# Linear output moved from routing to in front of the last projection, both it and the experts unrolled, first loads reordered

## The chip, the cores and the metric

The kernel runs on one core of a Trainium2 chip. The metric is the device time of one execution in microseconds. The kernel before takes 3159.98 us, the median of three runs from 3156.24 to 3162.64.

## The reference, cut to what matters

Two layers work on x, 4096 tokens (2 sequences of 2048) of 256 features.

```python
xn = layernorm(x)
# layer 0: linear attention beside a transformer block with experts
q_feat, k_feat = elu(rope(q) * hd**-0.5) + 1, elu(rope(k)) + 1
kv, k_sum = einsum('bhtd,bhtv->bhdv', k_feat, v), k_feat.sum(axis=2)
denom = maximum(einsum('bhtd,bhd->bht', q_feat, k_sum), 1e-6)
s = (einsum('bhtd,bhdv->bhtv', q_feat, kv) / denom[..., None]) @ W_out   # the "linear output"
#   the block: causal softmax attention (16 heads of 16), then 8 experts, two for a token,
#   1024 rows each: exp_out = gelu(rows @ W1 + b1) @ W2 + b2
g = silu(x1 + gate0 * exp_out[row0] + gate1 * exp_out[row1])
x = x + s * g
# layer 1: causal softmax attention with heads of 32 beside a quantised linear map
xn = layernorm(x)
s = attention(xn @ Wq, xn @ Wk, xn @ Wv) @ Wo
g = silu(xn @ int4(kernel) + bias + (xn @ a) @ b)
out = x + s * g
```

## The kernel before, in words

Tokens lie on the 128 partitions in 32 tiles, and a block is 4 tiles (512 tokens), so there are 8 blocks. A matrix product needs the features on the partitions, so rows are turned on TensorE first and evicted from PSUM by ScalarE. Stages follow one another, each its own block of the program: at its end all engines meet at a barrier, and POOL first drains its own queue (line 40).

1. `project_first` (tiles `pr_`, 0 to 269 us): layer norm, the linear attention's q, k, v, its features (`qf_all`, kept on the chip) and sums (`kv_sum`), and q, k, v of layer 0's softmax attention. Everything is unrolled and every engine follows a list of names (`pe_names`, `act_names`, `dve_names`). PSUM tiles of two banks come in turn from a ring of 3, and transposes (`Txn`, `Tz`, `soft`) from one more, `rot`. `Txn 0` can't start before ScalarE has copied the tables "soft cos", "soft sin" and "soft neg" out of `rot`. Statistics of the rows are taken in three groups of blocks: 0, then 1 to 3, then 4 to 7, the last of these in block 1.
2. `narrow_attention` (269 to 1095), `project_and_gate` (1099 to 1167).
3. `route_and_linear` (tiles `rl_`, 1167 to 1256.6): VectorE works out, in one chain, for each of 8 x 1024 expert rows which token it holds (`rows_at`). Between its links stand 16 calls of `normalise`, one for each pair of tiles of the linear output (10 ahead of `rows_at`, 6 behind it). For a pair, TensorE makes the numerators (`num`), VectorE divides by the denominators (L2125 is the first of its instructions), TensorE turns the result (`tr`, L2239), ScalarE copies it to `nT` (L2103), TensorE multiplies by W_out (`out`, L2251), ScalarE copies that, SyncE stores it in DRAM (`s_out`). Once `rows_at` is there (L2214), POOL issues 16 gathers (L2007) for experts 0 and 1.
4. `experts` (`ex_`, 1256.6 to 1738.1): loops over pairs of experts. For one: T (transposes of its rows, by halves of 4 tiles) into `xT`, h (8 x 2 products and gelu on ScalarE), y (128 products), an add on VectorE (L2401), and a store of POOL to `exp_out`, which POOL waits for.
5. `combine_and_project` (`p_`, 1738.2 to 2022): a loop over blocks. The expert rows of a block are gathered (L2545), mixed with the gates on VectorE (L2610, L2614), silu on ScalarE, times s (loaded back from `s_out`), plus x, layer norm, then TensorE's T (L2698), q and k (L2705), v (L2711) and y (L2718). q and k leave PSUM twice: the high half by ScalarE (L2577), the low half by VectorE (L2666). PSUM is a ring of 8 banks. `xT` is one buffer.
6. `wide_attention` (2022 to 3083.8) and `finish` (to 3153.7).

The names of steps carry block numbers, and an engine waits for another by the name of the step.

## Time and profile before

| what | us |
|---|---|
| median of 3 runs | 3159.98 (3156.24 to 3162.64) |
| the profiled execution's own time | 3155.44 |
| its span, first to last instruction | 3153.7 |
| TensorE busy | 2875.4 (91%) |
| VectorE / ScalarE / POOL busy | 2034.5 / 1545.4 / 953.3 |
| granted TensorE clock, mean | 0.951 of full |

A time in the rows below is read from the start of the span. `[3.63 <-ACT p_xT L2567]` behind an instruction says that its engine had been idle for 3.63 us, and what ended it. One line of a timeline can hold several instructions (x32), with the duration of all. PEclk is the granted TensorE clock: 1.00 is 2.4 GHz, 0.50 is 1.2 GHz.

### The profile page before, as it was taken

How to read it: one execution, taken by the hardware profiler on the slowest of the kernel's cores; microseconds unless marked ns; L12 is line 12 of the kernel's file. 1: busy time of each engine (PE TensorE's matmuls, PEld its weight loads, DVE VectorE, ACT ScalarE, POOL GpSimd, SP SyncE). 2: the span in 40 equal slices, each digit the busy share in tenths (PEclk: the TensorE clock that was granted, in tenths of full speed). 3: DMA queues.
4: the chain of work that ended last, by engine and by line, in shares of the span. 5: the costliest groups of instructions: out<-in, count | busy, mean ns of one | idle time of the engine just before them, and what ended most of it. 6: DMA issues, size and time to landing. Idle time of an engine off the chain costs nothing. (4 is left out here: it accounts for less than half of the span.)

```text
span 3153.7 us, 47934 instructions
## 1 busy us (share of the span) xinstructions
PE 2875.4 (91%) x18023; PEld 1334.8 (42%) x18023; DVE 2034.5 (65%) x4568; ACT 1545.4 (49%) x2562; POOL 953.3 (30%) x452
## 2 busy tenths in 40 slices
PE   7998999999999877999998588799999999999987
PEld 4664333333333256566666244323333333333326
DVE  6776899988999366000000465588877877878823
ACT  2442477776777732222221344344566565565560
POOL 0001000000000021211200221056777777777790
PEclk9997899999999978999999799889999999999998
DMA  4223121112220053222210445430220220202005
GB/s 121 84 64 88 34 45 42 23 37 45 48 42 15 23 160 98 66 61 68 85 47 20 145 148 185 125 71 5 64 61 8 65 50 22 61 21 55 8 8 173
DMA packets 149886, 204.29 MB, mean 65 GB/s; under 512 B 18224, under 2 KB 113280, under 8 KB 147744
## 3 DMA queue, kind: packets, MB, share of 16 engines
q1 hardware_dynamic: 129904, 170.76, 19.7%
q0 software_dynamic: 8704, 25.18, 3.0%
q10 hardware_dynamic: 11072, 5.60, 0.7%
q8 instruction: 130, 2.13, 0.3%
q14 instruction: 76, 0.62, 0.1%
HBM read 121.01 MB, written 79.95 MB: 64 GB/s over the span
## 5 line engine op out<-in xcount | busy, mean ns | idle before, releaser
L912 ACT ACTIVATE at_probs<-at_st 128x512 f32<-128x512 f32 (+3 forms) x1280 | 588.6, 541 | 446.0 <-PE at_st L998 283.9
L874 POOL TENSOR_TENSOR at_probs<-at_probs 128x2048 f32<-128x2048 f32 (+3 forms) x208 | 732.8, 3528 | 222.6 <-ACT at_probs L912 136.8
L383 DVE TENSOR_REDUCE at_part<-at_s 128x1 f32<-128x512 f32 (+3 forms) x1280 | 689.7, 603 | 69.9 <-PE at_s L421 31.7
L365 ACT ACTIVATE at_probs<-at_st 128x1024 f32<-128x1024 f32 (+3 forms) x640 | 541.5, 895 | 277.4 <-PE at_st L440 140.3
L938 DVE TENSOR_REDUCE at_part<-at_s 128x1 f32<-128x512 f32 x768 | 498.8, 683 | 69.0 <-PE at_s L990 65.0
L990 PE MATMUL at_s<-at_kT,at_qT 96*128 96x512 f16 (+3 forms) x1280 | 392.0, 362 | 28.4 <-DMA at_kT<-klo 10.4
L998 PE MATMUL at_st<-at_qT,at_kT 98*128 98x512 f16 (+3 forms) x1280 | 379.8, 356 | 15.4 <-ACT at_probs L912 10.7
L421 PE MATMUL at_s<-at_kT,at_qT 48*128 48x512 f16 (+3 forms) x1280 | 360.5, 367 | 26.1 <-DMA at_kT<-klo 9.8
L932 DVE CUSTOM_DVE_ANT_0 at_s<-at_s,at_later 128x384 f32<-128x384 f32 (+3 forms) x512 | 247.0, 498 | 110.1 <-PE at_s L990 109.7
L507 PE MATMUL at_acc<-at_probs,at_v 128*32 128x512 f32 (+3 forms) x2560 | 305.2, 551 | 8.9 <-ACT at_otile L352 8.8
L2401 DVE TENSOR_TENSOR ex_ot<-ex_bank,lin_b 128x512 f32<-128x512 f32 x32 | 22.1, 692 | 449.0 <-PE ex_bank L2431 449.0
L1059 PE MATMUL at_acc<-at_probs,at_v 128*32 128x512 f32 (+3 forms) x2560 | 288.4, 538 | 6.4 <-ACT at_otile L894 6.2
L440 PE MATMUL at_st<-at_qT,at_kT 50*128 50x512 f16 (+3 forms) x1280 | 283.0, 357 | 5.0 <-ACT at_probs L365 3.3
L1859 POOL TENSOR_TENSOR ag_a<-ag_a,ag_r 128x1024 f32<-128x1024 f32 x8 | 18.8, 2360 | 851.5 <-ACT ag_r L1876 851.5
L990 PEld LDWEIGHTS at_s<-at_kT,at_qT 96*128 96x128 f16 x1280 | 110.1, 98 | 355.6 <-DVE at_part L938 151.4
L421 PEld LDWEIGHTS at_s<-at_kT,at_qT 48*128 48x128 f16 x1280 | 100.1, 94 | 370.8 <-DVE at_part L383 317.7
L2431 PE MATMUL ex_bank<-lin_w,ex_hT 128*128 128x256 f32 x1024 | 224.5, 380 | 7.0 <-ACT ex_hT L2383 7.0
L2422 PE MATMUL ex_bank<-ex_xT,lin_w 128*128 128x512 f32 x512 | 223.7, 595 | 1.6 <-ACT ex_xT L2375 1.6
L2431 PEld LDWEIGHTS ex_bank<-lin_w,ex_hT 128*128 128x128 f32 x1024 | 193.9, 190 | 43.0 <-ACT ex_hT L2383 13.8
L998 PEld LDWEIGHTS at_st<-at_qT,at_kT 98*128 98x128 f16 x1280 | 123.0, 98 | 186.4 <-ACT at_probs L912 106.8
L2383 ACT ACTIVATE ex_hT<-ex_bank,ex_b 128x512 f32<-128x512 f32 x128 | 87.5, 687 | 232.4 <-PE ex_bank L2422 232.4
L2705 PE MATMUL p_bank<-p_xT,p_w 128*128 128x512 f32 x256 | 128.6, 666 | 28.8 <-ACT p_xT L2567 28.8
(320 smaller groups left out, 3256.4 us busy)
## 6 DMA issues: line engine op xcount, KB each, us to landing
att<-at_otile SPq DMA_DIRECT2D x64, 256.0 KB, 2.1
lin_w<-in_W SPq DMA_DIRECT2D x16, 1024.0 KB, 8.2
at_v<-v SPq DMA_DIRECT2D x14, 1024.0 KB, 14.5
v<-pr_vt SPq DMA_DIRECT2D x32, 256.0 KB, 3.2
exp_out<-ex_ot POOLq DMA_DIRECT2D x32, 256.0 KB, 2.6
v<-p_vt SPq DMA_DIRECT2D x32, 256.0 KB, 4.4
fi_a<-att SPq DMA_DIRECT2D x8, 1024.0 KB, 6.1
at_qT<-qhi SPq DMA_DIRECT2D x14, 512.0 KB, 9.2
```

The lines of the kernel that those rows point to most:

```text
L365: act.activation(probs[:, quad % RING, heads_down * p:heads_down * (p + 1), off:QB], st_ps[n % st_slots][:, :, off:QB], ACT.Exp, scale=EXP ...
L383: dve.tensor_reduce(part[:, w % 2, qt * HG + h, j:j + 1], s_ps[n % S_SLOTS][:, 0:width], AX.X, ALU.max).then_inc(item_free, 1)
L421: mm = pe.matmul(place[:, 0:width], QT[g % 2][rows, h // heads_down, q0:q0 + P], KT[g % 2][rows, h // heads_down, j * QB:j * QB + width], ...
L440: mm = pe.matmul(place[:, y, off:QB], KT[g % 2][rows, h // heads_down, kc * P:(kc + 1) * P], QT[g % 2][rows, h // heads_down, u * QB + off ...
L507: mm = pe.matmul(acc_ps[32 * h:32 * h + 32, off:QB], V[g % 2][:, kc, 32 * h:32 * h + 32], probs[:, quads % RING, h, off:QB], start=kc == 0 ...
L874: pool.tensor_tensor(total, total, probs[:, slots.slot[quad], :, off:QB], ALU.add).then_inc(add_done, 1)
L912: act.activation(probs[:, slots.slot[quad], h, off:QB], st_ps[n % ST_SLOTS][:, off:QB], ACT.Exp, scale=EXP_SCALE).then_inc(exp_done, 1)
L938: dve.tensor_reduce(part[:, w % 2, qt * HG + h, j:j + 1], s_ps[n % S_SLOTS][:, 0:width], AX.X, ALU.max).then_inc(item_free, 1)
L990: pe.matmul(place[:, 0:width], QT[g % 2][0:K, h, q0:q0 + P], KT[g % 2][0:K, h, j * QB:j * QB + width], start=True, stop=True).then_inc(ite ...
L998: mm = pe.matmul(place[:, off:QB], KT[g % 2][0:K + 2, h, kc * P:(kc + 1) * P], QT[g % 2][0:K + 2, h, u * QB + off:(u + 1) * QB], start=Tru ...
L1059: mm = pe.matmul(acc_ps[32 * h:32 * h + 32, off:QB], V[g % 2][:, kc, 32 * h:32 * h + 32], probs[:, slots.slot[quads], h, off:QB], start=kc ...
L2431: mm = pe.matmul(d[:, t * D:(t + 1) * D], hT[cb][:, n, (2 * m + t) * P:(2 * m + t + 1) * P], w2[k][:, n, :], start=n == 0, stop=n == NFF - 1)
```

## The change

**Routing.** `route` keeps only the chain to `rows_at`, the masked sums `kvd` and W_out (both now held on the chip until the last projection), and issues 4 gathers (expert 0, its first half) instead of 16. `normalise`, `turn`, `output`, the stores to `s_out` and the pairs' products and copies are gone from it.

**Experts.** The loops are unrolled. The other gathers are issued here, by halves with a semaphore each. T of expert e+1 stands between the last h of expert e and its last y. Expert 0 begins with T and h of its first half. SyncE issues the stores to `exp_out`, and POOL no longer waits for each.

**Last projection.** Unrolled. 11 pairs of the linear output stand in front of T 0, pairs 11 and 12 in front of block 0's products, 13, 14 and 15 in front of those of blocks 1 to 3. `s` and later `g` stay on the chip in `mix`, in the place of the features. Expert rows are mixed two blocks ahead, one instruction works on four tiles where that is possible, T of block b+1 stands ahead of y of block b, `xT` has two buffers, and PSUM is a ring of 3 tiles of two banks and `rot`.

**First projection.** Groups of statistics are blocks 0, 1, 2 to 3 (in block 1), 4 to 7 (in block 2). The table of `soft` and its 32 small transposes stand behind qkA 0 and qkB 0, in a load queue behind Wq and Wk. ScalarE takes xnT 0 and hT 0 first. The matrix `a` is loaded in rows by SyncE and turned on TensorE ("turn a") in block 2, instead of being loaded element by element by ScalarE's queue for block 1; `lora` and `levels` move from block 1 to 2.

**Ends of stages.** Experts and last projection free their semaphores with a clear and a second barrier.

```diff
-    NPRE, NLORA = 0, 1
-    groups_of = [(0, 1), (1, 4), (4, NB)]
-    pe_names = ["soft", "Txn 0", "Tz 0"]
-    act_names = ["sqrt 0", "turn 0", "turn 1", "soft cos", "soft sin", "soft neg", "xnT 0", "hT 0",
-                 "square f", "square 0", "square 1", "sqrt 1"]
+    NPRE, NLORA = 0, 2
+    groups_of = [(0, 1), (1, 2), (2, 4), (4, NB)]
+    counted_in = {1: 2, 2: 3}
+    pe_names = ["Txn 0", "Tz 0"]
+    act_names = ["sqrt 0", "xnT 0", "hT 0", "turn 0", "turn 1", "sqrt 1", "square f", "square 0", "square 1",
+                 "soft cos", "soft sin", "soft neg"]
...
         if b == NPRE:
-            pe_names += ["norm fq", "norm k"]
+            pe_names += ["soft", "norm fq", "norm k"]
+        if b == NLORA:
+            pe_names += ["turn a"]
...
-                act.dma_start(lora_aT[:, :], W["a"].rearrange("d r -> r d")).then_inc(kern_ld, 16)
...
-            for e in range(2):
-                gather_tokens(pool, z_rows, rows_at, xin, rows_ld, e)
+            gather_tokens(pool, z_rows, rows_at, xin, rows_ld, 0, 0)
...
-            for _ in range(PAIRS - 10):
-                normalise()
...
+                first(e, 1, range(half))
+                second(e, 0)
+                first(e, 1, range(half, NFF))
+                if e + 1 < E:
+                    turn(e + 1, 0)
+                    turn(e + 1, 1)
+                second(e, 1)
...
+    FIRST = 11
+    after_turn, after_v = {0: (11, 12), 1: (13,), 2: (14,), 3: (15,)}, {}
...
+            def lin(m):
+                pe_s.wait(act, f"nT {m}")
+                if m >= 2:
+                    pe_s.wait(act, f"s {m - 2}")
+                step(f"nT {m}", act.activation(nT[:, m % 2, :, :, :].rearrange("p t c n -> p (t c n)"),
+                                               rot.tile(f"nT {m}")[:, 0, :], ACT.Copy))
+                pe_s.wait(act, f"s {m}")
+                step(f"s {m}", act.activation(s_all[:, 2 * m:2 * m + 2, :].rearrange("p t n -> p (t n)"),
+                                              banks.tile(f"s {m}")[:, 0, :], ACT.Copy))
...
+            for m in range(6):
+                normalise(m)
+            mixed(0)
+            for m in range(6, 9):
+                normalise(m)
+            combine(0)
+            mixed(1)
+            for m in range(9, FIRST):
+                normalise(m)
+            normalised(0)
+            combine(1)
+            for b in range(NB):
+                for m in lin_of(b):
+                    normalise(m)
+                if b + 1 < NB:
+                    normalised(b + 1)
+                if b + 2 < NB:
+                    mixed(b + 2)
+                lower(0, "q", "A", b)
+                lower(0, "q", "B", b)
+                lower(1, "k", "A", b)
+                if b + 2 < NB:
+                    combine(b + 2)
+                lower(1, "k", "B", b)
...
+            for m in range(FIRST):
+                numerator(m)
+                if m:
+                    linear(m - 1)
+                    project(m - 1)
+            linear(FIRST - 1)
+            project(FIRST - 1)
+            turn(0)
```

## Rows read from the trace of the kernel before

**Rows 1.** Windows of routing and last projection: stretch, PE, PEld, DVE, ACT, POOL busy, PEclk, DMA, GB/s.
```profile
1167.00:1255.00 88.00, 62.91 (x388) 55.26 (x388) 61.85 (x224) 19.83 (x34) 15.50 (x16) 0.81 0.50 141
1734.00:2024.00 290.00, 221.12 (x576) 109.83 (x576) 148.65 (x369) 117.53 (x183) 62.84 (x66) 0.88 0.48 152
```

**Rows 2.** Timeline of routing and the start of the experts: start, duration, engine, line.
```profile
1176.00 0.26 DVE L2125 TENSOR_TENSOR rl_den<-rl_num,rl_least 128x16 f32<-128x16 f32 x2
1177.17 0.41 DVE L2167 SCALAR_TENSOR_TENSOR rl_G<-rl_hot,rl_G 128x256 f32<-128x256 f32 x1
...
1228.96 0.20 DVE L2214 CAST lin_rows_at<-rl_found 128x64 uint32<-128x64 f32 x1
1230.08 1.30 POOL L2007 DMA_INDIRECT lin_xin<-z_rows,lin_rows_at  x1 [81.37 <-DVE lin_rows_at L2214]
...
1249.20 0.95 POOL L2007 DMA_INDIRECT lin_xin<-z_rows,lin_rows_at  x1 [0.30 <-issue]
...
1259.06 3.34 ACT L2375 ACTIVATE ex_xT<-ex_bank,lin_gb 128x512 f32<-128x512 f32 x4 [0.21 <-PE ex_bank L2440]
```

**Rows 3.** Instructions of L40 on POOL's queue: lowest, mean, highest ns, first to last start.
```profile
L40 POOLq DRAIN  x1: 19802/19802/19802, 1236.6 to 1236.6; - x1
...
L40 POOLq DRAIN  x1: 6596/6596/6596, 1731.4 to 1731.4; - x1
```

**Rows 4.** Timeline of the end of the experts and the start of the last projection.
```profile
1727.76 0.69 DVE L2401 TENSOR_TENSOR ex_ot<-ex_bank,lin_b 128x512 f32<-128x512 f32 x1 [6.22 <-PE ex_bank L2431]
...
1738.21 0.38 SPq L2506 DMA_DIRECT2D p_xs<-in_x  x1
```

**Rows 5.** Waits in the experts: waiter, releaser, sum us, count, longest.
```profile
PE ex_bank L2431 <- ACT ex_hT L2383: 7.0, 8, 0.9
```

**Rows 6.** SyncE's semaphore instructions of L40 and L43, at two ends of stages.
```profile
L40 SPq EVENT_SEMAPHORE  x1: 17/17/17, 269.2 to 269.2; - x1
...
L43 SPq EVENT_SEMAPHORE  x1: 17/17/17, 269.8 to 269.8; - x1
...
L40 SPq EVENT_SEMAPHORE  x1: 17/17/17, 2022.0 to 2022.0; - x1
```

**Rows 7.** Timeline of one linear pair late in routing.
```profile
1236.68 0.60 PE L2239 MATMUL rl_tr<-all_identf,rl_nrm 128*128 128x128 f32 x4
1237.12 1.09 PE L2229 MATMUL rl_num<-rl_kvd,lin_qf_all 128*128 128x136 f32 x8
1237.37 0.59 ACT L2103 ACTIVATE rl_nT<-rl_tr 128x512 f32<-128x512 f32 x1
1238.05 1.89 PE L2251 MATMUL rl_out<-rl_w_out,rl_nT 128*128 128x256 f32 x8
```

**Rows 8.** Windows, columns as in group 1, in routing.
```profile
1236.00:1249.00 13.00, 13.00 (x76) 11.40 (x75) 3.09 (x14) 4.94 (x9) 9.85 (x11) 1.00 0.85 186
```

**Rows 9.** Waits in the last projection.
```profile
PE p_bank L2705 <- ACT p_xT L2567: 28.8, 8, 5.1
```

**Rows 10.** Timeline of TensorE in one block of the last projection.
```profile
1801.52 15.70 PE L2705 MATMUL p_bank<-p_xT,p_w 128*128 128x512 f32 x32 [3.63 <-ACT p_xT L2567]
1817.05 7.03 PE L2711 MATMUL p_bank<-p_w,p_xT 128*128 128x512 f32 x16
...
1828.03 1.09 PE L2698 MATMUL p_bank<-all_identf,p_z 128*128 128x128 f32 x8 [0.50 <-DVE p_z L2648]
```

**Rows 11.** A group of VectorE in the last projection: busy us, mean ns, idle before.
```profile
L2666 DVE SCALAR_TENSOR_TENSOR p_parts<-p_bank,all_score,p_parts 128x512 f16<-128x512 f32 x64 | 46.0, 748 | 97.1 <-ACT p_parts L2577 91.7 <-DVEq L1143 2.6 <-ACTq L1143 1.9
```

**Rows 12.** Timeline of the first 40 us.
```profile
11.51 1.38 DVE L1574 TENSOR_SCALAR all_x_all<-all_x_all,pr_mean,pr_rstd 128x256 f32<-128x256 f32 x4
...
20.58 1.94 PE L1715 MATMUL pr_rot<-all_identf,all_x_all 128*128 128x128 f32 x8 [7.08 <-ACT pr_table L1484]
```

**Rows 13.** Windows, columns as in group 1, blocks 1 and 2 of the first projection.
```profile
62.00:99.56 37.56, 31.13 (x126) 20.51 (x126) 31.97 (x61) 14.22 (x18) 0.00 (x0) 0.91 0.22 68
99.56:127.38 27.82, 27.16 (x122) 18.32 (x121) 21.78 (x26) 11.54 (x15) 0.00 (x0) 1.00 0.23 71
```

More of the change, by code:

```diff
@@ L1660, in _ @@
                     bounds()
-                if b == 1:
-                    statistics(2)
+                if b == NLORA:
+                    pe_s.wait(dve, "turn a")
+                    step("aT", dve.tensor_copy(lora_aT[:, :], banks.tile("turn a")[0:16, 0, 0:D]))
+                if b in counted_in:
+                    statistics(counted_in[b])
                 if b == 0:
@@ L1752, in _ @@
                     step("norm k", pe.matmul(d[:, 1, 0:NF], C["onesf"][:, :], gb2[:, :], start=True, stop=True))
+                if b == NLORA:
+                    pe.wait_ge(kern_ld, 48)
+                    d = banks.take(pe, "turn a")
+                    for f in range(NF):
+                        mm = pe.transpose(d[0:16, 0, f * P:(f + 1) * P], lora_a[:, f, :], ident[:, :])
+                    step("turn a", mm)
                 act_s.wait(pe, f"hT {b}")
@@ L2388, in _ @@
+            turn(0, 0)
+            gelu(0, 0, range(half))
+            turn(0, 1)
+            gelu(0, 0, range(half, NFF))
+            for e in range(E):
+                if e:
+                    gelu(e, 0, range(NFF))
+                gelu(e, 1, range(NFF))
+                if e + 1 < E:
+                    turn(e + 1, 0)
+                    turn(e + 1, 1)
         @block.vector
@@ new lines, in second @@
+            def second(e, cb):
+                act_s.wait(pe, f"h{cb}{NFF - 1} {e}")
+                for m in range(2):
+                    d = banks.take(pe, f"y{cb}{m} {e}")
+                    for t in range(2):
+                        for n in range(NFF):
+                            mm = pe.matmul(d[:, t * D:(t + 1) * D], hT[cb][:, n, (2 * m + t) * P:(2 * m + t + 1) * P],
+                                           w2[e % 2][:, n, :], start=n == 0, stop=n == NFF - 1)
+                    pe_s.step(f"y{cb}{m} {e}", mm)
@@ new lines, in combine @@
+            def combine(b):
+                cols = slice(4 * b, 4 * b + 4)
+                act_s.wait(dve, f"silu {b}")
+                act_s.wait(dve, f"s {2 * b + 1}")
+                link(tt(fg[:, b % 2, :, :], fg[:, b % 2, :, :], s_all[:, cols, :], ALU.mult))
+                dve.wait_ge(x_ld[b % 2], 16 * (b // 2 + 1))
+                step(f"x {b}", tt(x_all[:, cols, :], fg[:, b % 2, :, :], xs[b % 2][:, :, :], ALU.add))
+                dve_s.wait(dve, f"x {b}")
+                for t in range(4 * b, 4 * b + 4):
+                    last = dve.bn_stats(stats[:, t, :], x_all[:, t, :])
+                link(last)
+                moments(dve, link, stats[:, cols, :], mean[:, cols], var[:, cols], diff[:, cols])
+                step(f"moments {b}", dve.nop())
@@ L2689, in _, with numerator @@
         @block.tensor
         def _(pe):
-            pe_s.start(pe)
-            pe.wait_ge(w_ld, 80)
-            def body(blk, k, i, last):
+            step = pe_s.step
+            def numerator(m):
+                d = banks.take(pe, f"num {m}")
+                for y in range(2):
+                    t = 2 * m + y
+                    for f in range(NF):
+                        mm = pe.matmul(d[:, y, f * WID:(f + 1) * WID], mix[:, t, f, :], kvd[:, t // (NT // B) * NF + f, :],
+                                       start=True, stop=True)
+                step(f"num {m}", mm)
@@ new lines, in linear, with project @@
+            def linear(m):
+                dve_s.wait(pe, f"nrm {m}")
+                d = rot.take(pe, f"nT {m}")
+                for y in range(2):
+                    for f in range(NF):
+                        mm = pe.transpose(d[:, 0, (y * NF + f) * P:(y * NF + f + 1) * P],
+                                          nrm[:, m % 2, y, f * P:(f + 1) * P], C["identf"][:, :])
+                step(f"nT {m}", mm)
+            def project(m):
+                d = banks.take(pe, f"s {m}")
+                act_s.wait(pe, f"nT {m}")
+                for y in range(2):
+                    for f in range(NF):
+                        mm = pe.matmul(d[:, 0, y * D:(y + 1) * D], nT[:, m % 2, y, f, :], w_out[:, f, :],
+                                       start=f == 0, stop=f == NF - 1)
+                step(f"s {m}", mm)
```

906 lines of the change are left out of this document (431 added, 475 removed).

## The prediction

> **What bounds the kernel now.** First the page: TensorE is busy 91% of the span, so stages where it isn't are where time can be had, and the stages lie end to end, each closed by a barrier, so what one gains the next doesn't lose. Then the windows of the stages that the diff touches [rows 1]: in routing TensorE is busy 62.9 of 88 us, in the last projection 221 of 290, at clocks of 0.81 and 0.88. Then, in each stage, what ends it. Routing ends neither with TensorE nor with VectorE but with POOL: its 16 gathers begin 1.1 us behind `rows_at`, are 1.25 apart to 1249.20 [rows 2], and its drain lasts 19.8 from 1236.6, so to 1256.4 [rows 3], 7.2 behind the start of the last gather. Between experts and last projection nothing runs: VectorE's last add ends at 1728.45, the store is waited for, a drain of 6.6 follows from 1731.4, and the first load is issued at 1738.21 [rows 3, 4]. In the last projection TensorE waits for `xT` 8 times, 28.8 us in all [rows 9]; VectorE has 149 us of work in 290 and doesn't bind [rows 1].
>
> **Routing: -30.0.** The chain to `rows_at` loses 10 calls of `normalise`. One lies between 1176.00 and 1177.17 [rows 2] and costs 1.2: -12.0. The wait for the turned slot counts shrinks too, since on TensorE those stood behind pairs of 0.44 + 0.93 + 1.72 = 3.1 us, the starts of [rows 7]: one such pair gone is -3.0, with bounds of 0 and two pairs. So `rows_at` comes 15.0 earlier, at 1214.0, and the first gather at 1215.1. Four gathers instead of 16: the last starts 3 x 1.25 later plus the first one's extra, 1219.1. The drain ends 7.2 behind it, 1226.3, against 1256.4. The six `normalise` behind `rows_at` and the last stores were hidden by the gathers and are worth nothing here. The 12 gathers that move are issued by POOL in the experts, where it is idle; those of expert 0's second half are wanted only after T and half of h of the first, about 14 us on, and a gather took some 7 to drain. If that cover were gone, each gather late would cost its 1.25.
>
> **Experts: -9.5.** TensorE is at work nearly throughout; it waits at y for the last gelu 8 times, 7.0 us [rows 5]. Turning the next expert's rows between h and y covers seven of these: -6.1. The turned rows' own eviction, which now has y in front of it, gives -1.6 more by a second row of that view, so small that it isn't shown; bounds 0 and 3. At the start four evictions run one after the other in 3.34 [rows 2] before the first h; now two: -1.7. Unrolled loops have no more to give: the engine's queues are not what h and y wait for.
>
> **Between them: -5.8.** SyncE stores instead of POOL, so the drain of 6.6 [rows 3] finds nothing to wait for. From 1728.45 [rows 4]: about 3 until the last store has landed (1731.4, where the drain began, less the end of the add [rows 3, 4]), then the barrier. The clear and the second barrier cost 0.6, as between 269.2 and 269.8 [rows 6]. With 0.3 of barrier that is 3.9, where it was 9.76. Bounds: 0, if the drain costs the same however empty, and 6.6.
>
> **Last projection: +7.5.** Before, it lasts from 1738.21 to 2022.0, 283.8 [rows 4, 6], and holds no linear pair. I wrote the new order of the three engines out with the durations of before.
> A pair overlaps less than it did. In [rows 7] the next numerators fill the time in which ScalarE copies the turned rows (1237.37 to 1237.96). In the new order num m stands ahead of nT m-1, and s m-1 comes right behind, so TensorE waits 0.88 for the copy (0.59, and two hand-overs): 3.1 + 0.88 = 3.97 a pair, 43.7 for 11. Add 4 for the start at half clock, 1.6 for pair 6, held up by the mixing of block 0 on VectorE (8 instructions near 0.5), and 5.4 for pair 9, behind which stand combining block 0 and mixing block 1 (about 5.3 + 4 us, less what the ring has in hand, with some 1.2 for the clock afterwards). The pairs end at 54.7. T 0 is 0.9. Pairs 11 and 12 have nothing to overlap with: 0.93 + 1.25 + 0.44 + 0.6 + 1.72 and hand-overs of 0.5, 5.5 each. First q at 66.6.
> A block at full clock is 32 x 0.43 for q and k (16 of v take 6.87 net [rows 10]), 6.9 for v, 0.9 to 1.1 for T, 3.6 for y: 25.3. It was 31.2: T starts 26.5 behind the first q, and behind it come its own 1.1 and a wait of 3.6 for `xT`, after which the clock starts low [rows 10]. Now T b+1 is done and evicted under v and y. Blocks 0 to 2 carry the next block's pair with its full latency, 5.7: 31.0 each. Block 3: 25.3. Blocks 4 and 5: 26.4, since the low half of q waits behind mixing on VectorE, whose low-half pass costs 0.75 a bank and was already the engine's largest group [rows 11]. Then 25.3 and 24.4. 66.6 + 93.0 + 25.3 + 52.8 + 25.3 + 24.4 = 287.4, 3.2 for the last evictions and stores, 0.6 for the clear [rows 6]: 291.2, or +7.5. The bounds: TensorE alone, without a gap, has 251.5 + 4 of cold start (-28); every pair at 5.5 and every block at its old 31.5 would be 16 x 5.5 + 8 x 31.5 = 340 (+56). I take my list, nearer the lower, because both large waits have work put in front of them. The stores to and loads from `s_out` vanish, off the path.
>
> **First projection: +1.3.** `Txn 0` starts at 20.58, released by the tables; the row block that it turns is ready at 12.9 [rows 12], so it may start 7.6 earlier. The 32 small transposes now stand on TensorE between q, k and the norms, about 2 us: block 0 ends 6.0 earlier. Block 1 lasts 37.6 where block 2 lasts 27.8 [rows 13]: 9.7 more, from statistics of 16 tiles, levels and lora. It now has statistics of 8 tiles and no levels or lora: -3.0. Block 2 gets the other statistics, levels, `turn a`, lora: +10.3, the 9.7 of block 1 and 0.6 for the turn and its copy. Sum +1.3, between -4 (VectorE in block 2 is busy 21.8 of 27.8 [rows 13] and might take half of it unseen) and +4 (block 1's gain isn't there).
>
> **Sum.** +1.3 - 30.0 - 9.5 - 5.8 + 7.5 = -36.5. The profiled execution's own time is 3155.44, 1.7 over its span, and 4.5 under the median. Its successor would be 3119, and the median 3160 - 36.5 = 3123.5, say **3124**.
>
> **Rivals.**
> 1. The last projection doesn't reach TensorE's pace. The order silu, high half, low half makes a chain through ScalarE and VectorE with three PSUM tiles where there were 8 banks, so q waits for a low half in every block. For it: low halves already waited 91.7 us for high halves [rows 11]. Against it: neither engine has more than 19 us of work for a block of 25 [rows 1]. At 1.5 to 3 us a block: +12 to +24, 3136 to 3148.
> 2. The gain is larger: pairs at 3.1 (-14 over 16), or block 2 of the first projection absorbs its extra work (-5). For it: VectorE's idle time [rows 13]. Against: the order of the names. 3105 to 3115.
> 3. Slower, by one mechanism: the pairs run at 1.2 GHz. Each has a gap on TensorE of 0.88 in 3.97. In [rows 8] pairs run without a gap at a clock of 1.00; in the last projection, with a wait of 3.6 in each block, it is 0.88 in the mean [rows 1]. At half clock a pair's 3.1 become 6.2, so +3.1 each: all 16 are +50, 3174, and the kernel ends above 3160 from 12 slow pairs on; at 11 it is 3158, no change. Against it: TensorE would still be busy 78% of a pair's time.
> The Trainium skill, page "TensorE: Matmul & The Clock Gate", section "A second HAM failure mode: psum-queue depth-cycling", describes such a loss, micro-idles between groups of matmuls that cycle through PSUM banks; no stretch of this trace has such pairs with gaps, so it stays a rule against this order; by it the time would be rival 3's, 3158 to 3174.
> 4. The drain between the stages costs its 6.6 regardless, and gathers of the first half come late: 3132, inside the range.
>
> **Chances.** My forecast, 3115 to 3133: 0.60. Rival 1: 0.20. Rival 2: 0.11. Rival 3: 0.05 slower, 0.03 at no change. Beyond all of these 0.01. The range holds the forecast with most of rivals 1 and 2: 3110 to 3144. A measurement of this kernel can't tell 0.2%, 6.3 us, from no change. Faster 0.92, same 0.03, slower 0.05.
>
> **What would show it.** Routing: one POOL drain that ends near 1226, four L2007-like gathers, `rows_at` near 1214. Experts: from first to last instruction 462, and no row of TensorE waiting at y for the last gelu. Between: 4 us without work. Last projection: 11 pairs 3.97 apart at a clock of 1.00 but for the start, first q 67 us into the stage, blocks of 31, 31, 31, 25, 26, 26, 25, 24. First projection: Txn near 13, block 2 near 38. The forecast is wrong if a pair is over 5 us, if blocks without pairs take over 28, or if the clock in the pairs stands near 0.50.

## The result, and the profile after

The changed kernel takes 3110.89 us (median of 4 runs, 3104.42 to 3112.62), the kernel before 3159.44 beside it (4 runs): ratio 0.9843, 95% interval 0.9825 to 0.986. It is faster by 48.6 us where 36.5 were forecast; that is the low end of the range, 3110 (by the ratio on the 3159.44 it is 3109.8, a hair below). The profiled execution is the fastest of the four, with a span of 3102.5 against 3153.7, 51.2 less.

Cut at the barriers (SyncE's semaphore instructions of L40, as in [rows 6]), in us; the last column is what the terms of the forecast's sum say for the stage:

| stage | before | after | difference | forecast |
|---|---|---|---|---|
| first projection | 269.2 | 268.7 | -0.5 | +1.3 |
| routing | 89.6 | 54.4 | -35.1 | -30.0 |
| experts, with the closing barrier | 481.6 | 463.2 | -18.4 | -15.3 |
| last projection | 283.8 | 289.8 | +6.0 | +7.5 |
| the four stages that weren't touched | 2029.5 | 2026.3 | -3.2 | 0 |

The 3 us of the untouched stages are chance: the same kernel run again (below) has them back, 831.5, 69.8, 1061.9 and 69.7, 2033 in all, and its gain was 46.

**Routing.** The timeline and, of the drain, the instructions of L40:
```profile
1210.60 0.20 DVE L2175 CAST lin_rows_at<-rl_found 128x64 uint32<-128x64 f32 x1
1211.72 1.30 POOL L2034 DMA_INDIRECT lin_xin<-z_rows,lin_rows_at  x1 [65.67 <-DVEq L40]
...
1215.84 0.94 POOL L2034 DMA_INDIRECT lin_xin<-z_rows,lin_rows_at  x1 [0.30 <-issue]
...
1222.25 8.06 PE L2339 MATMUL ex_bank<-ex_xT,lin_w 128*128 128x512 f32 x15 [0.96 <-ACT ex_xT L2285]
```
```profile
L40 POOLq DRAIN  x1: 5937/5937/5937, 1212.8 to 1212.8; - x1
```
The first gather starts 47.2 us behind the stage's barrier where it was 63.1 [rows 2], so 15.9 sooner (forecast 15.0). The last of four starts 4.1 later, and the drain ends at 1218.8, 2.9 behind the start of the last gather. It was 7.2 in [rows 2, 3], and 7.2 was carried over in the forecast. What VectorE waits for in the chain, before and after:
```profile
DVE rl_found L2213 <- PE rl_rt L2266: 3.6, 1, 3.6
```
```profile
DVE rl_found L2174 <- PE rl_rt L2193: 0.4, 1, 0.4
```
This is the wait for the turned counts, 3.2 less (forecast 3.0), and VectorE is busy for 41.5 us up to `rows_at` instead of 53.9, 12.3 less (forecast 12.0).

**Experts.** Waits from the first h to the end:
```profile
PE ex_bank L2339 <- ACT ex_xT L2285: 1.0, 1, 1.0
PE ex_bank L2349 <- ACT ex_hT L2292: 0.8, 1, 0.8
```
The 7.0 of [rows 5] are 0.8. TensorE's timeline, the fourth quarter of h of two experts:
```profile
1259.00 7.03 PE L2339 MATMUL ex_bank<-ex_xT,lin_w 128*128 128x512 f32 x16
...
1315.84 7.03 PE L2339 MATMUL ex_bank<-ex_xT,lin_w 128*128 128x512 f32 x16
```
From one expert to the next it is 56.84 us; before, the same step recurs every 58.47. Seven boundaries at -1.63 are -11.4. The first h begins 3.3 behind the barrier instead of 4.8 (-1.5), but from there to the fourth quarter's first matmul it takes 36.75 instead of 35.06 (+1.7): the second half's T now stands in between, and the first quarter, still at a low clock, lasts 8.5 instead of 7. Sum -11.2.

**Between them.** Timeline:
```profile
1678.89 0.69 DVE L2319 TENSOR_TENSOR ex_ot<-ex_bank,lin_b 128x512 f32<-128x512 f32 x1 [6.21 <-PE ex_bank L2349]
1682.69 0.37 SPq L2485 DMA_DIRECT2D p_xs<-in_x  x1
```
The last add ends at 1679.58 and the first load is issued 3.1 later. In [rows 4] it was 9.76; the forecast said 3.9.

**Last projection.** TensorE's timeline (the idle time before an instruction and its releaser in brackets), then windows with the columns of [rows 1], three of the last projection behind the stage's own and two of the first projection at the end:
```profile
1702.84 0.60 PE L2707 MATMUL p_rot<-all_identf,p_nrm 128*128 128x128 f32 x4
1704.22 1.97 PE L2716 MATMUL p_bank<-mid_w_out,p_nT 128*128 128x256 f32 x8 [0.78 <-ACT p_nT L2530]
1706.02 1.09 PE L2698 MATMUL p_bank<-mid_kvd,all_mix 128*128 128x136 f32 x8
...
1728.68 0.66 PE L2707 MATMUL p_rot<-all_identf,p_nrm 128*128 128x128 f32 x4 [3.65 <-DVE p_nrm L2605]
1730.12 3.65 PE L2716 MATMUL p_bank<-mid_w_out,p_nT 128*128 128x256 f32 x8 [0.78 <-ACT p_nT L2530]
...
1736.84 1.04 PE L2725 MATMUL p_rot<-all_identf,p_z 128*128 128x128 f32 x8
...
1746.04 0.66 PE L2707 MATMUL p_rot<-all_identf,p_nrm 128*128 128x128 f32 x4 [1.46 <-DVE p_nrm L2605]
1747.48 3.55 PE L2716 MATMUL p_bank<-mid_w_out,p_nT 128*128 128x256 f32 x8 [0.78 <-ACT p_nT L2530]
1750.87 13.90 PE L2751 MATMUL p_bank<-p_xT,p_w 128*128 128x512 f32 x32
1764.60 7.03 PE L2759 MATMUL p_bank<-p_w,p_xT 128*128 128x512 f32 x16
1771.47 1.04 PE L2725 MATMUL p_rot<-all_identf,p_z 128*128 128x128 f32 x8
1772.34 3.62 PE L2769 MATMUL p_bank<-p_w_ffn,p_xT 128*128 128x256 f32 x16
```
```profile
1682.00:1972.00 290.00, 259.81 (x896) 154.09 (x896) 155.44 (x345) 117.41 (x129) 61.12 (x64) 0.98 0.43 138
1690.00:1711.00 21.00, 17.11 (x106) 15.03 (x106) 9.92 (x28) 6.42 (x12) 12.04 (x14) 1.00 0.47 151
1724.00:1737.00 13.00, 7.74 (x35) 6.02 (x34) 12.31 (x36) 6.11 (x8) 7.24 (x8) 0.87 0.22 61
1747.00:1751.00 4.00, 3.52 (x9) 2.90 (x10) 3.89 (x11) 0.33 (x1) 0.00 (x0) 0.57 0.00 0
56.00:89.00 33.00, 28.94 (x121) 19.22 (x120) 26.71 (x47) 14.28 (x18) 0.00 (x0) 0.95 0.22 66
89.00:127.00 38.00, 31.47 (x131) 20.85 (x130) 32.27 (x62) 14.53 (x19) 0.00 (x0) 0.91 0.22 67
```
A pair runs from one projection to the next (the groups of 0.60, 1.97 and 1.09), 4.11 us apart, with a gap of 0.78 for ScalarE's copy, at a clock of 1.00. Pair 9 waits 3.65 for VectorE, and the projection behind it then runs at half clock (3.65 instead of 1.97; 0.87 in the window). Pair 12's projection runs at half clock too (3.55; 0.57), with no wait as long in front of it: in pairs 11 and 12 TensorE waits 1.46 for VectorE and 0.78 for ScalarE each, in 5.8 us. The eleven pairs end 54.1 behind the stage's first load, the first q starts at 68.2, and the blocks last 30.92, 30.91, 30.92, 24.93, 25.58, 25.59, 24.93 and 24.2. T stands between v and y with no gap before it: the 28.8 us of [rows 9] are gone.

**First projection.** TensorE's timeline:
```profile
12.77 1.94 PE L1736 MATMUL pr_rot<-all_identf,all_x_all 128*128 128x128 f32 x8 [12.77 <-DVE all_x_all L1589]
...
89.24 7.03 PE L1728 MATMUL pr_bank<-pr_wl,pr_xnT 128*128 128x512 f32 x16
...
111.00 3.89 PE L1728 MATMUL pr_bank<-pr_wv,pr_xnT 128*128 128x264 f32 x8 [5.87 <-DVE pr_turned L1607]
```
`Txn 0` starts 7.8 sooner than in [rows 12]. Block 1 ends 10.3 sooner against the start, block 2 lasts 37.7, with 5.87 of waiting for VectorE's rotation in the middle of v.

### The profile page after: what moved, and what is told of

It reads as the page before. It is cut to its first block and busy times, and to the rows that moved or that the text cites. A ratio compares the mean times of both kernels' runs of the same rounds, so it can differ in the third digit from the quotient of the medians.

```text
span 3102.5 us, 46462 instructions
## 1 busy us (share of the span) xinstructions
PE 2850.2 (92%) x18025; PEld 1325.8 (43%) x18025; DVE 2022.6 (65%) x4462; ACT 1520.9 (49%) x2473; POOL 929.4 (30%) x420
## 5 line engine op out<-in xcount | busy, mean ns | idle before, releaser
L421 PE MATMUL at_s<-at_kT,at_qT 48*128 48x512 f16 (+3 forms) x1280 | 359.6, 366 | 26.4 <-DMA at_qT<-qhi 10.2
L2034 POOL DMA_INDIRECT lin_xin<-z_rows,lin_rows_at x64 | 60.9, 951 | 297.3 <-PE ex_bank L2330 211.4
```

What stands on the lines that cost most here:

```text
L421: mm = pe.matmul(place[:, 0:width], QT[g % 2][rows, h // heads_down, q0:q0 + P], KT[g % 2][rows, h // heads_down, j * QB:j * QB + width], ...
```

## The experiments

Two theories stood at the start. Mine: the terms are right but for the drain, which depends on how many gathers and stores are still under way when POOL reaches the end of its block. The rival: the gain comes from TensorE itself, unrolled loops and a better clock, and the drain is a fixed price. Each kernel below is the changed one with one edit (the cuts of code show its main part), timed against the kernel before on the same chip. "Stage" times are of the profiled execution, cut as in the table.

**The changed kernel again**, no edit.

> The changed kernel again, untouched, as the measure for the others and for how much the stages move between executions. In its first profile the stages that the diff leaves alone (both softmax attentions, the gate, the last stage) were together 3.5 us shorter than before. If that is chance, they come out anywhere within about 4 us of before here, and the median stays at 3105 to 3113. If the change really shortened them (other addresses on the chip, another clock at their start), they are 3 to 4 us shorter again.

3113.1, ratio 0.9857 (0.9841 to 0.9873). Routing 54.3, experts 464.1, last projection 289.5: the three terms repeat to 1 us, the luck of the long stages doesn't. It is the base for the next three.

**All 16 gathers in routing again.**
```diff
-            gather_tokens(pool, z_rows, rows_at, xin, rows_ld, 0, 0)
+            for e, cb in ((0, 0), (0, 1), (1, 0), (1, 1)):
+                gather_tokens(pool, z_rows, rows_at, xin, rows_ld, e, cb)
...
-            for e, cb in ((0, 1), (1, 0), (1, 1)):
-                gather_tokens(pool, z_rows, rows_at, xin, rows_ld, e, cb)
```


> The changed kernel with all 16 gathers of experts 0 and 1 in routing, as before; there are still no linear pairs and no stores to s_out in it. First theory, the tail of POOL's drain is the backlog of 16 gathers: 12 x 1.25 = 15.0 more for the issues and a drain that ends 7.2 behind the last gather instead of 2.9, routing 54.4 -> 73.7 us, +19.3. Rival, the tail was made by the stores of the linear output, which shared the queues: the drain ends 3 us behind the last gather as with four, routing 69.4, +15.0. The experts don't change in either.

3130.93, ratio 0.9905 (0.9888 to 0.9921), 17.8 above the base; routing 71.7, 17.4 more. POOL's timeline and the drain:
```profile
1239.53 0.95 POOL L2034 DMA_INDIRECT lin_xin<-z_rows,lin_rows_at  x1 [0.31 <-issue]
```
```profile
L40 POOLq DRAIN  x1: 17857/17857/17857, 1227.0 to 1227.0; - x1
```
The drain ends at 1244.86, 5.3 behind the last gather's start. Twelve more gathers cost 12 x 1.25 = 15.0 of issue and 2.4 of longer tail. So the truth lies between the two theories. The tail is the landing of the last gather: from issue to landing it took 2.7 us in the changed kernel, 4.6 here and 6.5 before, and each drain ended 0.2 to 0.7 behind that landing. Between 5.3 and the 7.2 of before lie 1.9; the linear output's work and its stores to `s_out` are what those two routings differ by. The kernel before itself, run on another chip (c2_before, below), bears this out. There ScalarE stood still, so that SyncE issued no store beside the last nine gathers, the last of which started at 1255.78, and the drain ended 5.3 behind that one, at 1261.1:
```profile
L40 POOLq DRAIN  x1: 17972/17972/17972, 1243.1 to 1243.1; - x1
```
So of the 4.3 that the forecast missed, 2.4 are the backlog of gathers, shown by the edit; 1.9 go with the stores under way, by what differs and by this one trace.

**T of the next expert behind y again.**
```diff
+                second(e, 1)
                 if e + 1 < E:
                     turn(e + 1, 0)
                     turn(e + 1, 1)
-                second(e, 1)
```


> The changed kernel with the turned rows of the next expert behind the last y again, still unrolled. The experts take 460.6 us from their start to the last add, 471.9 before. First theory, the place of T is what pays: TensorE waits again at the last gelu and at the turned rows, +6.8 to +7.5. Rival, unrolling paid for most of it: +3 or less. If both hold their part, about 3 of the 11.3 us gained belong neither to this nor to the shorter start (1.6).

3126.35, ratio 0.989 (0.9873 to 0.9906), 13.3 above the base; experts 474.2 against 464.1, more than either theory said. From one expert to the next it is 58.40 us: 1.56 more than with T in its new place, of which the idle rows show 0.78 + 0.27. The code is unrolled here too, and as a loop it took 58.47, so it is the place of T that pays; unrolling is worth 0.07 a boundary. Its last projection, which has the same code, took 296.1 instead of 289.5: TensorE stood at half clock for 8 us near its start, where the base has 0.79 in the mean:
```profile
1696.00:1704.00 8.00, 7.31 (x26) 6.42 (x27) 2.62 (x9) 0.60 (x1) 5.68 (x6) 0.50 0.84 305
```
That is a measure for chance: one profile of this stage, unchanged, gives anything from 289.5 to 296.1 on a chip of this kind.

**The experts' stores on POOL again.**
```diff
+                for cb in range(2):
+                    for m in range(2):
+                        dve_s.wait(pool, f"y{cb}{m} {e}")
+                        pool.dma_start(rows[e, cb, m], ot[:, cb, m, :, :]).then_inc(stored[2 * cb + m], 16)
+                        pool.wait_ge(stored[2 * cb + m], 16 * (e + 1))
...
```


> The changed kernel with the experts' output stored by POOL, which waits for each store, as before. First theory: from the last add to the last projection's first instruction 3.1 -> 9.7 us, as before, +6.6, since POOL's drain after the store costs 6.6 whatever else there is. Rival: the drain was long because a store by POOL was fresh in a queue shared with gathers; as SyncE's part it is the same kernel otherwise, and the gap is 5 us or less. The rest of the experts doesn't change in either, since POOL's gathers run two experts ahead.

3115.55, ratio 0.9862 (0.9845 to 0.9878), 2.5 above the base, which the noise of the medians could hide; the profile shows it directly. Timeline and L40 of its POOL:
```profile
1680.50 0.69 DVE L2318 TENSOR_TENSOR ex_ot<-ex_bank,lin_b 128x512 f32<-128x512 f32 x1 [6.21 <-PE ex_bank L2348]
1681.73 0.71 POOL L2272 DMA_DIRECT2D exp_out<-ex_ot  x1 [6.18 <-DVE ex_ot L2318]
1687.50 0.37 SPq L2484 DMA_DIRECT2D p_xs<-in_x  x1
```
```profile
L40 POOLq DRAIN  x1: 2356/2356/2356, 1684.5 to 1684.5; - x1
```
From the add's end (1681.19) to the first load it is 6.3: 3.2 of the 6.7 come back, and the drain is 2.4, not the 6.6 of [rows 3], although here too POOL's gathers were long done. So 3.2 of this term is the store on POOL. The other 3.4 stay unexplained: this experiment doesn't bring them back. The traces say where they sit. The store lands 2.8 us behind the add in the kernel before and 3.1 here; then the drain is 4.2 shorter here, and the clear at the stage's end adds 0.5. Neither theory held.

**The first projection, old and in between.** Four kernels; they ran on chips where the kernel before took 3171.31 (first two), 3172.80 and 3169.22.

Whole function as before (groups of statistics 0, 1 to 3, 4 to 7; old loads and order):

> The changed kernel with the first projection of before (its order of loads, its groups of statistics, lora in block 1), except that its features go to the shared buffer and the frequency table shares room with two working tiles. The first profile says that the new one is 0.5 us shorter in all: block 0 ends 5.9 earlier, block 1 4.5 shorter, block 2 9.9 longer. First theory: the new first projection is worth nothing, +0.5 here, 3111. Rival: the new start does more than it shows, by leaving the loads less crowded, +3 or more.

3135.31, ratio 0.989 (0.9874 to 0.9906). The stage lasts 269.6, against 268.5 and 268.8 in two kernels with the new one on that chip. The new first projection gains about 1 us here, where +1.3 was forecast; but over all profiles the same new code took 268.0 to 269.9, so a gain isn't shown.

Statistics block by block, each ahead of the second rotation:
```diff
-    groups_of = [(0, 1), (1, 2), (2, 4), (4, NB)]
-    counted_in = {1: 2, 2: 3}
+    groups_of = [(0, 1), (1, 2), (2, 4), (4, 5), (5, 6), (6, 7), (7, NB)]
+    counted_in = {1: 2, 2: 3, 3: 4, 4: 5, 5: 6}
...
```


> The changed kernel with the statistics of blocks 4 to 7 taken one block at a time in blocks 2 to 5, instead of all in block 2. First theory: the 9.9 us that block 2 costs over a plain block are VectorE's statistics (16 tiles of 0.35, 5.6 us) standing ahead of the second rotation while TensorE waits for PSUM; a quarter of it in each of four blocks fits in VectorE's 6 idle us, so -4 to -8. Rival: each block then pays for its own chain of small instructions and two table loads of 1.28 us on ScalarE, and it is slower by 4 x 2 us.

3132.9, ratio 0.9883 (0.9864 to 0.9901). The stage takes 270.6, 2 more: block 2 falls from 37.7 to 32.1, but blocks 3 to 5 rise from 27.8 to 30.4 each, since v waits in every one:
```profile
138.54 2.05 PE L1728 MATMUL pr_bank<-pr_wv,pr_xnT 128*128 128x264 f32 x8 [1.77 <-DVE pr_turned L1607]
```
Same groups, the statistics at the end of VectorE's block instead (`counted_in` becomes {1: 2}, and groups 3 to 6 stand behind `lo k`, their square root ahead of `xnT` on ScalarE):

> The changed kernel with the statistics of blocks 4 to 7 one block at a time in blocks 2 to 5, behind the low halves of k, where VectorE waits 2.5 us for the sums of TensorE in each block, instead of ahead of the second rotation. In the first such try, ahead of the rotation, block 2 became 5.6 shorter and blocks 3 to 5 2.6 longer each. Theory: it is the place ahead of the rotation that costs; here blocks 3 to 5 lose at most 1 each and the first projection is 3 to 6 us shorter, 263 to 266. Rival: the chain statistics, square root on ScalarE, inverse root, normalise is late for the next block's transposes there too, and it is as long as now, 268.7 or more.

3152.21, ratio 0.9933 (0.9921 to 0.9946): 17.4 slower than the changed kernel beside it, the stage 287.1. The chain of moments, square root and copy stands before the next block's first matmul (waits in blocks 3 to 5):
```profile
PE pr_rot L1749 <- ACT pr_xnT L1485: 16.1, 3, 5.4
```
New start, but all statistics, levels and lora in block 1 as before:
```diff
-    NPRE, NLORA = 0, 2
-    groups_of = [(0, 1), (1, 2), (2, 4), (4, NB)]
-    counted_in = {1: 2, 2: 3}
+    NPRE, NLORA = 0, 1
+    groups_of = [(0, 1), (1, 4), (4, NB)]
+    counted_in = {1: 2}
...
```


> The changed kernel with the start of the new first projection (the frequency table late, ScalarE's new order) but the old groups of statistics (0, 1 to 3, 4 to 7 in block 1), levels and lora in block 1. Theory: the parts add. The new start is worth 5.9; blocks 1 and 2 take 33.1 + 37.7 = 70.8 in the changed kernel and 37.5 + 27.8 = 65.3 before; so 5.5 less, the first projection 263.2. Rival: with three blocks of rows in the second load the weights come later and block 0 takes back 3 or more of it.

3127.18, ratio 0.9865 (0.985 to 0.988), 3.7 under the changed kernel beside it; the stage 262.6, so 6.8 less. The stage is clear, the median isn't (the intervals overlap): the unchanged `narrow_attention` behind it took 836.2 in this profile and 830.9 in the other, and it wanders from 827.5 to 836.8 in kernels with the new first projection as it is. The early start is worth its 6 us only if the work isn't moved: in block 2 the same work takes the gain back.

**The pairs' gap filled**, on the chip of the first two of these. The numerators of pair m + 2 between nT m and s m:
```diff
+            numerator(0)
+            numerator(1)
             for m in range(FIRST):
-                numerator(m)
-                if m:
-                    linear(m - 1)
-                    project(m - 1)
+                linear(m)
+                if m + 2 < FIRST:
+                    numerator(m + 2)
+                project(m)
```


> The changed kernel with the numerators of pair m+2 between the turned rows and the output product of pair m, for the 11 pairs in front. The profile has a pair each 4.11 us, 0.78 of it TensorE waiting for ScalarE's copy plus the time at which matmuls don't overlap. First theory: the gap is filled, 3.1 us a pair as late in routing, 9 pairs x 1.0 = -9. Rival: with three tiles in the ring the output product of m now waits for the normalised rows of m+1 and the gap moves there, 0 to -3.

3127.12, ratio 0.9862 (0.9844 to 0.9879); last projection 301.7, against 304.6 and 305.0 in the two kernels beside it with the unchanged one: -3, which a stage that wanders like this one can't show.

**All 16 pairs in front.**
```diff
-    FIRST = 11
-    after_turn, after_v = {0: (11, 12), 1: (13,), 2: (14,), 3: (15,)}, {}
+    FIRST = 16
+    after_turn, after_v = {}, {}
```


> The changed kernel with all 16 pairs in front of the last projection instead of 11 in front and 5 in the blocks. A pair in front costs 4.11 us, one in a block 5.8 (30.9 against 25.1 without). First theory: 5 x 1.7 = -8.5. Rival: T 0 and the first q then come 20 us later and blocks 0 to 2 meet the mixing of later blocks as blocks 4 and 5 do, +0.7 each, and the mixing of block 0 holds the pairs up as it does now: -6 or less.

3127.42, ratio 0.9871 (0.9852 to 0.989); last projection 298.0: -7. By the medians this kernel and the one before it are the same.

**Both edits**, with the changed kernel beside it, on another chip.

> The changed kernel untouched, beside the three that follow. Four kernels of the second set ran on a chip on which the kernel before took 3171 instead of 3159 us, and there the unchanged last projection took 305 us instead of 290, the unchanged experts 469 instead of 463, with the missing time in waits of 2 to 9 us early in the last projection in which ScalarE and VectorE stood still although what they wait for was there. Theory: it is the chip (on such a one the last projection is near 305 again, on one as the first near 290). Rival: it was the kernels' own layout, and here it is 290 whatever the chip.

> All 16 pairs in front, and the numerators of pair m+2 between the turned rows and the output product of pair m. Beside the changed kernel: moving five pairs to the front gave 7 us of the last projection, filling the gap 3 us. Theory: both are independent of each other, 15 pairs x 0.3 and 7, -10 to -12. Rival: with the gap filled TensorE meets VectorE's mixing earlier and waits there, so that the sum is no more than the larger of the two, -7.

3134.77 and 3120.47; ratios 0.988 (0.9866 to 0.9894) and 0.9829 (0.9816 to 0.9842). The last projection goes from 308.3 to 291.8. Together they gain 16.5 in the stage and 14.3 in the time, more than 3 and 7 added. Part of that is the base: two more kernels on this chip whose last projection is the unchanged one (e9 and e10) have it at 304.7 and 304.4, and against them it is 13. The rest is open.

**Why do the chips differ?** Where the kernel before takes near 3170, the changed kernel gains 38 us; where it takes 3159, 46 to 49. The changed kernel in this set, timeline of three engines and windows:
```profile
1713.16 0.95 POOL L2517 DMA_INDIRECT p_rows<-exp_out,all_gather_at  x1 [0.30 <-issue]
1714.04 0.60 ACT L2533 ACTIVATE all_mix<-p_bank 128x512 f32<-128x512 f32 x1 [7.82 <-remote]
1716.88 0.19 DVE L2600 TENSOR_TENSOR p_den<-p_bank,p_least 128x32 f32<-128x32 f32 x1 [11.47 <-remote]
...
1717.68 3.75 PE L2716 MATMUL p_bank<-mid_w_out,p_nT 128*128 128x256 f32 x8 [7.99 <-ACT p_nT L2530]
```
```profile
1693.00:1701.00 8.00, 6.56 (x24) 5.88 (x25) 2.69 (x9) 0.60 (x1) 5.12 (x6) 0.50 0.75 267
1701.00:1722.00 21.00, 11.09 (x49) 9.27 (x49) 2.60 (x8) 2.92 (x5) 10.05 (x11) 0.74 0.44 143
```
ScalarE is idle for 7.8 us and VectorE for 11.5, and the trace names no instruction that released them. That says little: on the three chips with a standstill the traces have no landing for any gather. Here are the gathers of the experts in the DMA view of e0_again and of this run; the last number, where there is one, is the us from issue to landing:
```profile
lin_xin<-z_rows,lin_rows_at POOLq DMA_INDIRECT x64, 3.2
```
```profile
lin_xin<-z_rows,lin_rows_at POOLq DMA_INDIRECT x64
```
So a releaser can be missing from the record. The standstill itself is in the times. It ends near the last of POOL's 16 gathers, and TensorE's clock is 0.50 before and 0.74 around it. The end is no accident. In the eleven changed kernels profiled on these chips the later of the two engines goes on 3.7 to 4.1 us behind the start of the 16th gather (here 1716.88 behind 1713.16), wherever it had stopped. Suspected: the weights' load, or the gathers. The weights after pair 3:
```diff
             load_x(0)
+            pe_s.wait(sp, "s 3")
             for n, name in enumerate(("Wq", "Wk", "Wv")):
```


> The changed kernel with the weights of q, k, v (1.5 MB) and all loads behind them asked for only when pair 3 is done, about 17 us into the last projection; they are wanted at 68. Theory: ScalarE and VectorE stood still because the transfers of their own instructions queued behind 3 MB of loads and 16 gathers that kept all queues busy for 15 us, so with half of it later the last projection is near 290 on any chip. Rival: the instructions' transfers aren't hindered, the standstill is the same, and where the chip shows none nothing changes (0 within 1).

3136.19, ratio 0.9884 (0.9869 to 0.9899); last projection 304.6, and VectorE stands still for 11.5 again: not the weights. The standstill ends 3.8 behind the 16th gather, as in the others. The kernel before against itself, and the changed kernel beside it:

> The kernel before, untouched, for its profile. On the chip of the second and third set the changed kernel gained 38 us instead of 46: its experts take 469 instead of 463 us and its last projection 305 to 308 instead of 290, while the kernel before took 3172 instead of 3159. Theory: both unrolled stages lose to late instruction transfers, which loops don't need; so where the kernel before takes about 3172, its own experts and last projection are as long as on the first chip (481.5 and 283.9) and its 13 us lie elsewhere. Rival: its experts and last projection are longer there too, by some 13 us together.

> The changed kernel untouched, beside the others of this set. By the theory above: on a chip with the kernel before at 3159 it takes 3113 with a last projection of 290, on one with 3172 it takes 3134 with one of 305 to 308.

3169.23, ratio 1.0003 (0.9994 to 1.0012), and 3130.87, ratio 0.9883 (0.9868 to 0.9899). The kernel before stands still too, but in routing (timeline):
```profile
1255.78 0.95 POOL L2007 DMA_INDIRECT lin_xin<-z_rows,lin_rows_at  x1 [0.30 <-issue]
1258.02 0.60 ACT L2094 ACTIVATE rl_ot<-rl_out 128x512 f32<-128x512 f32 x1 [12.10 <-remote]
...
1259.50 0.26 DVE L2125 TENSOR_TENSOR rl_den<-rl_num,rl_least 128x16 f32<-128x16 f32 x2 [8.02 <-remote]
```
Here too VectorE goes on 3.7 behind the start of the last gather. The stage takes 100.0 instead of 89.6, its looped experts and last projection 481.8 and 283.6, within 0.5 of the table. The changed kernel has 54.3 in routing, but 468.8 in the experts (463.2) and 303.9 in the last projection (289.8). In the experts TensorE waits 2.4 to 3.9 us for a late gelu some 30 us into the stage in all eleven profiles from these chips, right behind a series of 20 gathers. So the loss moved with the unrolled pairs and the series of gathers beside them. Then the second eight gathers held back until `nrm 5`, alone and with the late weights:
```diff
                 if b >= 2:
                     dve_s.wait(pool, f"mixed {b - 2}")
+                elif n == 4:
+                    dve_s.wait(pool, "nrm 5")
```


> The changed kernel with POOL's second eight gathers of the last projection (block 1's rows) asked for when pair 5 is normalised instead of straight behind the first eight. On the slower chip ScalarE and VectorE stood still for 8 to 12 us in the third pair, and in four profiles went on within 1 to 3 us of the end of POOL's first series of 16 gathers (20 us long); in the kernel before's routing on that chip it is the same. Theory: on such a chip their next instructions arrive only when the series ends, so with a series of 8 (10 us) the standstill ends some 10 us earlier or is gone, and the last projection takes 292 to 298 instead of 304 to 308. Rival: the two ends fall together by chance, the standstill stays where it was and the stage at 304 or more. Mixing block 1 must not become late: it starts 40 us into the stage, these gathers end about 36 us into it. On a chip like the first nothing changes (289.5).

> The same with the weights of q, k and v and all loads behind them late too, behind pair 3 (which alone changed nothing: 304.6). Theory of the gathers: like the run beside it within 1 us, since loads of this kind don't matter. Rival, that it takes a crowd of both: with the late gathers alone the standstill stays, and it goes only here.

3116.8 and 3118.16; ratios 0.9851 (0.9832 to 0.9869) and 0.986 (0.9841 to 0.9879); last projection 293.8 in both, and nowhere a standstill. But this chip has the kernel before at 3163.45 and experts at 463.8, near the table's 463.2: the changed kernel wouldn't have stood still there either, as far as can be told, and the two runs decide nothing. The fixed distance to the end of the series speaks for the gathers; no edit has shown it, and by what means they would hold the two engines up stays open.

**The best of what was found**: both edits of the last projection and the in-between first projection.

> That first projection together with all 16 pairs in front and the filled gaps. Beside the changed kernel of this set: -5.5 and -14.3 (what the latter gave in the third set), -20 in all, if they don't touch each other, as they are 1400 us apart. On the first chip that would be about 3095, on the other 3115. Rival: the gain of the filled gaps was partly that of a chip that stood still anyway, and on the first chip the two give -15.

3113.52, ratio 0.9824 (0.9811 to 0.9837), 17.4 under the changed kernel on the same chip, whose interval it doesn't touch. It beats both kernels there. ScalarE and VectorE stand still in it too, for 12.8 and 9.3 us. None of the kernels with filled gaps, all pairs in front or the in-between first projection ran on a chip without the standstill, so what they gain there isn't known.

## Why the prediction was right and where it was wrong

**Routing, the step that failed.** "The drain ends 7.2 behind it" took the tail as a constant of the last gather. It grows with what is under way: 2.9 with 4 gathers, 5.3 with 16, 7.2 with 16 and the stores. That is 4.3 of the 5.1 by which the term was short; 0.9 is the chain to `rows_at`, -15.9 for -15.0, and the trace has both of its parts, -12.3 of VectorE's work for -12.0 and -3.2 of waiting for -3.0. So the ten `normalise` and one pair's wait were the right account. That the other six and the 12 moved gathers cost nothing held on the first chip: TensorE didn't wait for T of the second half there.

**Experts.** -11.2 for -9.5. The waits were the right ones: all but 0.8 of the 7.0 went, and putting T back cost 10. The size was off at the boundaries, -11.4 for -6.1 - 1.6 = -7.7. An idle row undercounts a stall: groups of matmuls back to back overlap in the trace (1704.22 + 1.97 is 1706.19, and the next starts at 1706.02), so a gap of 0.87 is worth 0.87 + 0.17 = 1.04, and the one behind T 0.4. The other 0.2 of the 1.63 are the groups behind the gaps, which ran 0.1 shorter each. Putting T back shows it a second time: idle rows of 1.05 a boundary, a price of 1.56. Against it, the start gave nothing (-1.5 + 1.7) where -1.7 was set: the forecast counted the evictions and left out that T of the second half still has to run, a little later.

**Between.** -6.7 for -5.8, and the price right for half of the reason: 3.2 are the store's queue, 3.4 aren't explained.

**Last projection.** +6.0 for +7.5. Each line of the list is near: pairs 4.11 for 3.97 (0.78 and twice 0.17, where 0.88 was set), their end 54.1 for 54.7, first q 68.2 for 66.6, blocks 30.9, 24.9, 25.6 and 24.2 to 24.9 for 31, 25.3, 26.4 and 24.4 to 25.3. The clock fell where a wait of 3.65 was foreseen, and once more in pair 12, which wasn't: its 1.6 are about what the first q is late by. That +6.0 lies so near is one profile's luck in part: other profiles of this code on such chips are 289.5 to 296.1. Rival 1 is refuted: inside q and k TensorE waits for a low half in blocks 4 and 5 alone, 0.39 each. Rival 3, pairs at half clock, is refuted on the first chip for the pairs in front.
The Trainium skill, page "TensorE: Matmul & The Clock Gate", section "A second HAM failure mode: psum-queue depth-cycling", describes a kernel whose clock went down and up again because TensorE was idle for short moments between groups of matmuls. Rival 3 rested on such gaps. Here the pairs' gaps of 0.78 in 4.11 left the clock at 1.00, so for the pairs in front the measurement decides against it. For the two that stand by themselves, with 1.46 and 0.78 in 5.8, it came true once, at 1.6 us.

**First projection.** -0.5 for +1.3. Block 0 -5.9 (said -6.0), block 1 -4.4 (-3.0), block 2 +9.9 (+10.3): the decomposition was right to 1.4. The pure exchange of the two versions gives -1, no more than the spread of one version.

**Rival 2**, a larger gain, is where the time landed, but not by either of its mechanisms: the pairs took 4.11, not 3.1, and block 2 absorbed nothing. What was missing is a sum of small misses of one sign: 5.1 for routing, 1.7 for the experts, 0.9 between them, 1.5 and 1.8 for the projections make 11.0 of the 12.1 between the forecast and the measured gain. All five lean the same way, and that puts the time at the very edge of the range.

## What to carry over

Before a barrier, count what POOL's queue still holds: each indirect gather that can be issued behind the barrier gives back its issue time and some of the drain's. A stall that repeats costs more than its idle row by the overlap that the stalled matmuls lose, here 0.17 us each time, so read the period from start to start. And work that an early start leaves over must go where VectorE has slack in that very block: spread over blocks that were just balanced, the same statistics cost 2 us in one place and 18 in another. Compare the time of one stage only after seeing it several times unchanged: on the disturbed chips the last projection took 303.9 to 308.3 with one and the same code.

## What the hardware showed unexpectedly

- POOL's drain at the end of a block follows the landing of its last gather by 0.2 to 0.7 us: it ends 2.9 behind the start of the last of 4, and 5.3 behind the last of 16. With all landed it still lasts 2.4 us in one kernel (e3) and 6.6 in another (the kernel before); why isn't known.
- On three of the chips ScalarE and VectorE stand still together, mostly for 6 to 14 us, in unrolled code beside a series of 16 gathers, and go on 3.7 to 4.1 behind the start of the last; the traces there hold no landing of the gathers, and no releaser. It cost the kernel before about 10 us in routing, the changed one 14 to 18 in the last projection and 5 to 6 in the experts. Keeping weights away didn't help; the cause wasn't found.
- ScalarE changes its function table between the last projection's pairs. Two of these loads (timeline of the changed kernel):
```profile
1724.76 1.28 ACT L2542 ACT_TABLE_LOAD   x1
1726.05 0.20 ACT L2542 ACTIVATE p_std<-p_var 128x4 f32<-128x4 f32 x1
1726.27 1.28 ACT L2538 ACT_TABLE_LOAD   x1
1727.57 1.06 ACT L2538 ACTIVATE p_fg<-p_fg 128x1024 f32<-128x1024 f32 x1
```
The activation starts 1.29 and 1.30 behind the start of a load that lasts 1.28, so nothing comes on top. The Trainium skill, page "ScalarE: Activation LUTs", section "What ACT_TABLE_LOAD costs", adds a pipeline drain of about 1.38 us to a load; it doesn't show here.
